# A convolution by five products: the last product added onto the third one in PSUM

## The reference

```python
def _L1_conv_ref(x, w1, w3, w5, wd, wf):
    x1 = _conv(x, w1, padding=[(0, 0), (0, 0)])
    x2 = _conv(x, w3, padding=[(1, 1), (1, 1)])
    x3 = _conv(x, w5, padding=[(2, 2), (2, 2)])
    x4 = _conv(x, wd, padding=[(2, 2), (2, 2)], dilation=(2, 2))
    out = jnp.concatenate([x1, x2, x3, x4], axis=1)
    return _conv(out, wf, padding=[(0, 0), (0, 0)])
...
x = x + _L0_conv_ref(_gn(x), ...)
x = x + _L1_conv_ref(_gn(x), ...)
```

## Time and profile before

| | us |
|---|---|
| Median of three runs | 1710.36 |
| The three runs | 1708.89, 1710.36, 1710.79 |
| Span of the profiled execution | 1706.1 |

### The profile page before, as it was taken

The page is one execution under the profiler, slowest core; times in us unless marked ns, Lnnn a source line. Parts: engine busy times, 40 slices in busy tenths (PEclk is TensorE's granted clock), DMA queues, the critical chain, the costliest instruction groups (busy, mean ns, idle before and its releaser), DMA issues.

```text
span 1706.1 us, 38231 instructions
## 1 busy us (share of the span) xinstructions
PE 1652.5 (97%) x13285; PEld 1552.1 (91%) x13285; DVE 1488.7 (87%) x1964; ACT 1022.2 (60%) x1665; POOL 579.8 (34%) x398
## 2 busy tenths in 40 slices
PE   6999999999999999999999999999999999999998
PEld 6989959999999996999999996899999999599998
DVE  6788879999888859999978886999988887799997
ACT  4856576555385658545546666755446566765551
POOL 4999931222281003232247002123326400312222
PEclk9999979999999997999999999899999999799999
DMA  7012115666502201666630220366661121055553
GB/s 192 0 47 65 38 32 136 177 164 172 153 2 61 69 19 44 157 167 172 169 95 15 69 65 1 87 165 175 167 165 46 35 73 41 1 133 139 135 144 104
DMA packets 105017, 166.01 MB, mean 97 GB/s; under 512 B 40266, under 2 KB 78763, under 8 KB 104780
## 3 DMA queue, kind: packets, MB, share of 16 engines
q1 hardware_dynamic: 81772, 138.95, 32.0%
q10 hardware_dynamic: 23168, 26.04, 4.7%
HBM read 52.20 MB, written 25.17 MB: 45 GB/s over the span
## 4 chain that ended last, share of the span: by engine, by line
PE 84%; DVE 7%; issue 4%; ACT 3%; DMA 1%; DVEq 0%; SPq 0%; POOL 0%; ACTq 0%; POOLq 0%
PE ps L957 41%; PE ps L796 12%; PE ps L817 8%; PE ps L819 7%; PE ps L818 7%; PE ps L845 3%; PE ps L879 3%; PE ps L952 1%; PE ps L752 1%; ACT region L1178 1%; DVE region L1706 1%; DVE region L1676 1%; ACT region L1111 1%; DVE X L1514 1%; DVE region L1673 1%
## 5 line engine op out<-in xcount | busy, mean ns | idle before, releaser
L957 PE MATMUL ps<-region,W 128*96 128x256 f16 (+2 forms) x7140 | 800.7, 270 | 10.0 <-DMA region<-region 5.4
L957 PEld LDWEIGHTS ps<-region,W 128*96 128x96 f16 (+1 forms) x7140 | 771.3, 122 | 31.8 <-issue 14.8
L1428 DVE TENSOR_TENSOR region<-V,band 128x2322 f32<-128x2322 f32 (+2 forms) x104 | 257.8, 2488 | 59.5 <-PE ps L819 56.1
L1178 ACT ACTIVATE region<-region 96x1584 f16<-96x1584 f32 (+2 forms) x80 | 98.4, 1272 | 309.1 <-DVE region L1610 309.1
L701 POOL TENSOR_TENSOR region<-region 96x528 f32<-96x528 f32 (+1 forms) x72 | 92.0, 1282 | 445.9 <-DVE region L1676 328.4
L817 PE MATMUL ps<-region 128*128 (+1 forms) x1152 | 228.1, 280 | 10.4 <-DVE region L1428 4.5
L819 PE MATMUL ps<-region 128*128 (+1 forms) x1152 | 222.8, 275 | 0.0
L818 PE MATMUL ps<-region 128*128 (+1 forms) x1152 | 222.2, 274 | 0.0
L1706 DVE SCALAR_TENSOR_TENSOR region<-ps,small,region 96x768 f32<-96x768 f32 (+1 forms) x220 | 203.7, 988 | 12.1 <-PE ps L957 10.4
L796 PE MATMUL ps<-proj,region 96*128 96x240 f32 x1024 | 209.3, 367 | 0.6 <-DVE region L1402 0.6
L796 PEld LDWEIGHTS ps<-proj,region 96*128 96x128 f32 x1024 | 194.8, 191 | 14.1 <-DVE region L1402 1.0
(11 more groups left out here) (234 smaller groups left out, 2199.8 us busy)
## 6 DMA issues: line engine op xcount, KB each, us to landing
region<-region SPq DMA_DIRECT2D x104, 247.5 KB, 3.9
region<-in_x_dram SPq DMA_DIRECT2D x128, 192.0 KB, 2.3
out_dram<-region SPq DMA_DIRECT2D x40, 576.0 KB, 4.2
region<-region ACTq DMA_DIRECT2D x72, 247.5 KB, 2.4
X<-in_x_dram SPq DMA_DIRECT2D x30, 576.0 KB, 6.2
region<-region SPq DMA_DIRECT2D x32, 247.4 KB, 4.9
X<-in_x_dram SPq DMA_DIRECT2D x19, 384.0 KB, 10.6
region<-region SPq DMA_DIRECT2D x24, 185.6 KB, 3.7
```

The lines of the kernel that those rows point to most:

```text
L957: last = mm(o, w, src, start=k == 0, stop=k == len(steps) - 1, skip_group_check=split and ck > 0)
L1178: act.activation(dst[0:C, a:e, x:z], src, ACT.Copy, scale=1.0 if whole else col(SA)).then_inc(s_h, 1)
L1428: v.tensor_tensor(T[:, i, 3 * c:3 * c + m].rearrange("p m (i j) -> p m i j", j=3), taps.broadcast_to([P, m, BW // 3, 3]), mask.broadcast_t ...
```

## The change

The weights of g4 are made 1.5 times as large. g4 then adds onto g2's banks, once VectorE has read g2 for the output rows 0 and 1 out of three; the row 2 takes g2 + 1.5 g4 in one step, with the factor 2/3 that g2 had there, so VectorE's step for g2 in row 2 is gone. The even units use the banks 6 for g0, g2 and g4, the odd ones 0; g1 has 2 for itself and g3 has 4. The waits of PE, ACT and DVE are counted anew, with 10 steps of a unit in place of 11. g4's low matmul takes 128 rows; the rows 64 to 127 of its weights are zero. ScalarE's first copy moves from behind the two sums to ahead of them. POOL's weight split has one more step, the factor 1.5.

```diff
-    BANKS = ((0, 2, 0, 4, 6), (2, 0, 2, 4, 6), (0, 2, 0, 4, 2))
+    PAIRS_OF = ((6, 2, 6, 4, 6), (0, 2, 0, 4, 0))
...
-        NPL, NH, NL, NCV, NACC = 8, 8, 4, 5, 11
+        NPL, NH, NL, NCV, NACC = 8, 8, 4, 5, 10
...
                 columns(0, h[0])
-                columns(2, h[2])
+                step(pool.tensor_scalar(early, h[2], 1.5, None, ALU.mult))
+                columns(2, early)
...
-                        pe.wait_ge(s_acc, (b * UNITS - 1) * NACC + (5, 9, 8, 0)[i] + START)
+                        if b:
+                            pe.wait_ge(s_acc, (b * UNITS - 1) * NACC + (-2, 2, 7, 8)[i] + START)
...
+                            if not first:
+                                pe.wait_ge(s_acc, (n - 2) * NACC + 8 + START)
+                        elif g == 1:
                             pe.wait_ge(s_acc, (n - 1) * NACC + 2 + START)
-                        elif g == 1:
-                            pe.wait_ge(s_acc, (n - 1) * NACC + 5 + START)
                         elif g == 2:
                             pe.wait_ge(s_t1, n + 1 + START)
                         elif g == 3:
-                            pe.wait_ge(s_acc, (n - 1) * NACC + 8 + START)
-                        elif last_unit:
-                            pe.wait_ge(s_acc, n * NACC + 2 + START)
-                        else:
-                            pe.wait_ge(s_acc, (n - 1) * NACC + 9 + START)
+                            pe.wait_ge(s_acc, (n - 1) * NACC + 7 + START)
+                        elif g == 4:
+                            pe.wait_ge(s_acc, n * NACC + 4 + START)
...
+                            opens = g < 4 and (g != 2 or column // BANK not in cleared)
+                            cleared.add(column // BANK)
...
                             if ck == 0:
-                                rows = 64 * len(rts)
-                                steps.append((wp[0:rows, p, :], window(lo, rows, 0, 0)))
+                                steps.append((wp[:, p, :], window(lo, P, 0, 0)))
...
-                                last = mm(o, w, src, start=k == 0, stop=k == len(steps) - 1, skip_group_check=split and ck > 0)
+                                last = mm(o, w, src, start=opens and k == 0, stop=k == len(steps) - 1,
+                                          skip_group_check=g in (2, 4) or split and ck > 0)
...
                         plain(hi, 1)
                         plain(hi, 0)
+                        between()
                         act.wait_ge(s_pl, later(b, u) * NPL + START)
                         sums(hi, 0)
                         sums(hi, 1)
...
                     act.wait_ge(s_cv, n * NCV + 1 + START)
-                    act.wait_ge(s_acc, (n - 1) * NACC + 7 + START)
+                    act.wait_ge(s_acc, (n - 1) * NACC + 6 + START)
...
                     def midway():
-                        if whole > 1:
-                            first_point(m, i, BPU)
                         if ahead:
                             rows_normed(m + 2, ahead)
...
-                    highs(m + 1, 1 - i, whole, midway)
+                    highs(m + 1, 1 - i, whole, midway, lambda: first_point(m, i, BPU))
...
                     step(1, 2, OSC_THIRD, 1)
-                    step(2, 2, OSC_THIRDS, 2)
...
-                    step(2, 4, OSC)
+                    step(2, 4, OSC_THIRDS)
```

More of the change, by code:

```diff
@@ L146, in build_program, with product_at, product @@
         ps = ctx.enter_context(nc.psum_tensor("ps", [P, 8, BANK], f32))
+        products = ps[0:C].rearrange("p b n -> p (b n)")
+        def product_at(i, g):
+            return PAIRS_OF[i][g] * BANK
+        def product(i, g, blocks):
+            at = product_at(i, g)
+            return products[:, at:at + 3 * KCOL].rearrange("p (c n) -> p c n", c=3)[:, :, 0:blocks * HC]
         pq = region[:, 0:2 * AR * CO].rearrange("p (i r c) -> p i r c", i=2, r=AR)
@@ L336, in build_program @@
         N_TURNED = 3 * (3 + 2) + 1
-        N_SPLIT = 12 + NRT * 6 + 2
+        N_SPLIT = 13 + NRT * 6 + 2
         NPOOL = 18
@@ L886, in _, with unit @@
                 keep_warm(0, 22)
-                def unit(u, i, k2, first, blocks, last_unit=False, halves=False):
+                def unit(u, i, k2, first, blocks, halves=False):
                     n = b * UNITS + u
@@ L892, in unit @@
                     for g, p in enumerate(POINTS):
-                        bank = BANKS[2 if last_unit else i][g]
+                        place = product_at(i, g)
                         if g == 0:
@@ L924, in unit @@
                         split, late = g == 0 or (first or halves) and g == 2, []
+                        cleared = set()
                         for c, ck in enumerate((1, 2, 0)):
-                            o = ps[0:C, bank:bank + 2, :].rearrange("p b n -> p (b n)")[:, ck * KCOL:ck * KCOL + blocks * HC]
+                            column = place + ck * KCOL
+                            o = products[:, column:column + blocks * HC]
+                            opens = g < 4 and (g != 2 or column // BANK not in cleared)
+                            cleared.add(column // BANK)
                             def window(t, rows, second, x):
@@ L964, in _ @@
                     unit(k2 * 2 + 1, 1, k2, False, BPU)
-                unit(UNITS - 1, 0, (UNITS - 1) // 2, False, LASTB, True)
+                unit(UNITS - 1, 0, (UNITS - 1) // 2, False, LASTB)
                 assert st.n == NPST
@@ L1161, in rows_normed, with highs @@
                                    ACT.Identity, bias=col(SBI), scale=col(SA)).then_inc(s_y2, 1)
-                def highs(u, i, whole, midway):
+                def highs(u, i, whole, midway, between=None):
                     n = b * UNITS + u
@@ L1231, in first_point @@
                     n = b * UNITS + u
-                    bank = BANKS[i][0]
                     act.wait_ge(s_cv, n * NCV + 1 + START)
-                    act.wait_ge(s_acc, (n - 1) * NACC + 7 + START)
-                    act.activation(acc[:, 1, :, 0:blocks * HC],
-                                   ps[0:C, bank:bank + 2, :].rearrange("p b n -> p (b n)")[:, 0:3 * KCOL]
-                                   .rearrange("p (c n) -> p c n", c=3)[:, :, 0:blocks * HC],
+                    act.wait_ge(s_acc, (n - 1) * NACC + 6 + START)
+                    act.activation(acc[:, 1, :, 0:blocks * HC], product(i, 0, blocks),
                                    ACT.Copy, scale=col(OSC_MHALF)).then_inc(s_t1, 1)
@@ L1695, in lows @@
                         sums(1, 4)
[L1697 to L1700, removed]
                 def first_rows(u, i, blocks):
@@ L1726, in last_rows @@
                     dve.wait_ge(s_cv, n * NCV + 4 + START)
-                    dve.wait_ge(s_acc, n * NACC + 7 + START)
+                    dve.wait_ge(s_acc, n * NACC + 6 + START)
                     step(0, 3, OSC_HALF)
                     dve.wait_ge(s_cv, n * NCV + 5 + START)
-                    step(2, 4, OSC)
+                    step(2, 4, OSC_THIRDS)
                 def outputs(u, blocks, rows):
@@ L1741, in middle_outputs @@
                     n = b * UNITS + u
-                    dve.wait_ge(s_acc, n * NACC + 5 + START)
+                    dve.wait_ge(s_acc, n * NACC + 4 + START)
                     dve.wait_ge(s_out, n * 16 + START)
@@ L1746, in outer_outputs @@
                 def outer_outputs(u, blocks):
-                    dve.wait_ge(s_acc, (b * UNITS + u) * NACC + 9 + START)
+                    dve.wait_ge(s_acc, (b * UNITS + u) * NACC + 8 + START)
                     outputs(u, blocks, slice(0, 3, 2))
@@ L1777, in _ @@
                 outer_outputs(UNITS - 2, BPU)
-                first_rows(UNITS - 1, 2, LASTB)
-                dve.wait_ge(s_acc, (b * UNITS + UNITS - 1) * NACC + 5 + START)
+                first_rows(UNITS - 1, 0, LASTB)
+                dve.wait_ge(s_acc, (b * UNITS + UNITS - 1) * NACC + 4 + START)
                 rows = X[:, (UNITS - 1) * UR * W:].rearrange("p (r j c) -> p c r j", j=HC, c=2)
@@ L1786, in _ @@
                 middle_outputs(UNITS - 1, LASTB)
-                last_rows(UNITS - 1, 2, LASTB)
+                last_rows(UNITS - 1, 0, LASTB)
                 outer_outputs(UNITS - 1, LASTB)
```

## The result

The changed kernel takes 1698.98 us (median of five runs, 1698.17 to 1701.03). The kernel before, run beside it, takes 1709.94 us. The ratio is 0.9939, with a 95% interval of 0.9927 to 0.9951: 11 us faster. The forecast was 1697.6 us, with a range of 1694 to 1705.

A forecast was written before the change was run, and what follows sets the result against it. VectorE's loop was taken to set PE's pace; 1706.1 us of span less 12.8 us (3.2 us an image, four images) gives 1693.3, plus 4.3 us from span to median makes 1697.6 us; range 1694 to 1705.

The forecast's parts named there:

- VectorE's loop bounded the kernel before: Steady units before: VectorE releases ScalarE's first copy, which releases PE, so PE runs at VectorE's pace, 18.95 us a unit.
- The 64-row matmul costs 0.26 us: PE, low matmul of g4: three steps around it take 0.59 us where 0.33 is regular; 128 rows save 0.26 us.
- The rival that this cost isn't its height: PE, 64-row matmul: its extra cost has another cause and stays, units 18.79 us, total 1707 us; chance 0.05.
- PE's unit becomes 18.53 us: Steady units after the change: PE needs 167 matmuls by 0.111 us, 18.53 us, and becomes the bound.
- VectorE has 0.51 us a unit to spare: VectorE's loop: one step of 0.926 us less takes it from 18.95 to 18.02 us, 0.51 us below PE's unit.
- The loop of the output's write: VectorE's middle outputs waiting for the previous unit's write: a loop of 17.5 us, below 18.53, so it costs nothing.
- g4's new wait is paid once: PE, g4 waiting for VectorE's two reads of g2: 2.6 us idle in unit 0 of each image, nothing afterwards.
- The rival of shared banks paid in every unit: PE at g4: both reads of g2 stand bare each unit, 20.5 us a unit, total 1758 us; chance 0.02.
- The clock falls at unit 0: Rival, PE behind g4's new idle: half of some 20 us lost, 10 us an image, 1718 to 1738 us; chance 0.06.
- The copy moved, and the looser waits: ScalarE's first copy ahead of the sums, and looser waits at g0, g1 and the next image: both cost nothing.
- POOL's extra step: POOL's weight split, once: one step of 2.7 us, covered by 14.74 us of POOL idle behind the split.
- The sum: Per image -0.2, +3.3 from eight units, +0.1: 3.2 us gained; four images 12.8 us.

The follow-up runs named there:

- the copy back: Changed kernel with ScalarE's first copy back behind the two sums: 1698.34 us, ratio 0.9927; with matmuls filling unit 0's idle as well, 1694.88 us.
- the warming matmuls: Changed kernel with identity matmuls into a free bank ahead of g4's wait in unit 0: 1696.70 us, ratio 0.9917; again 1695.99 us, ratio 0.9915.
- POOL's other order: Changed kernel with POOL's second difference issued ahead of its residual instead of behind it: 1702.59 us, ratio 0.9957.
- VectorE's first rows ahead: Changed kernel with VectorE's four steps for unit 0 moved ahead of its last two low parts of unit 1: 1704.06 us, ratio 0.9970.

## Why the prediction was right, and where a term was off

- **VectorE's loop bounded the kernel before, and the two edits need each other.** Right. With the 128 rows alone the units stay at 18.95 us; with the VectorE step alone (the 64 rows back) they are 18.79.
- **The 64-row matmul costs 0.26 us.** Right: 18.79 us with it, 18.53 without, in every steady unit. The rival that this cost isn't its height is out.
- **PE's unit becomes 18.53 us.** Right to the hundredth.
- **VectorE has 0.51 us a unit to spare.** Wrong, and the one step of the working that failed. The step priced the removed instruction by its own 0.926 us and moved everything behind it forward at its old duration. The plane step then lay 0.63 us beside POOL's difference and grew by 0.49 us. Where POOL isn't beside it, the loop is the 18.02 us of the forecast (18.03 in image 1). The gaps of 0.5 us on VectorE that were to show the step right aren't there, except where it waits for the write of the output (0.56 us above) and, with 0.28 us, in the last image with the copy back. The time was right all the same, because VectorE's 18.51 us are still just below PE's 18.53. The forecast had no ground for these 0.02 us, so that much is luck. The loop of the output's write, counted at nothing, is late by such amounts too. PE doesn't see it in the first profile of the changed kernel; with the warming matmuls it did, by 0.20 and 0.36 us in two units.
- **g4's new wait is paid once.** Right: 2.6 us of idle forecast in image 0, 2.43 measured, and 1.59 to 2.30 in the others; the wait at unit 1's g2 went as forecast, and no wait at g4 breaks PE from unit 1 on in the changed kernel's first profile. The reason given, that VectorE gains 0.51 us a unit, isn't the one: as I read it, and no run tests it by itself, two loops of equal length keep the phase that unit 1 leaves them. POOL's other order, which puts VectorE 0.21 us above PE, shows the wait in steady units at once. The rival of shared banks paid in every unit is out. The Trainium skill's "Perfetto Trace Analysis", Optimizing Tensor Performance, Matmuls, would have groups rotate through banks; in the changed kernel three of the five products share one pair, and PE is busy 148.24 of 148.24 us, because other products lie between them.
- **The clock falls at unit 0.** This rival, with a chance of 0.06, came true in its mechanism and not in its price, and with it one of the forecast's signs of being wrong, a clock below 1.00 behind unit 0. It was priced at half of some 20 us, from the stretch in the attention; the stretch here is 3.4 us, 1.6 us an image, in one to three images of four. In the six traces with this idle and no warming matmuls it fell in 12 of 24 images; in the four where warming matmuls shorten the idle it fell in none of 16. So the fall comes with the long idle, but not each time. The Trainium skill's "TensorE: Matmul & The Clock Gate", Part 1, says that idling brings the low clock back, and the traces agree in 12 of the 17 images whose idle at g4 was 1.88 us or longer.
- **The copy moved, and the looser waits.** Nothing, as forecast. **POOL's extra step** took 3.6 us against 2.7, and POOL still idles 13.19 us behind the split against 14.74, so its cover held.
- **The sum.** 3.2 us an image were forecast; an image whose clock stays up gains 205.4 - 202.35 = 3.05 us, so 12.2 us in all. The falls take back 1.6 to 4.7 us. The three medians of the changed kernel, each against the kernel before beside it, give 11.0, 13.2 and 10.2 us, while the convolutions of the three traces gain 7.8, 11.0 and 8.1 us. The other 2 to 3 us aren't explained by the change: the span without the convolutions is 884.1 to 887.3 us in the thirteen traces, whatever the kernel, and 884.5 us in the only trace of the kernel before, whose execution was 2 us below its median. So it is in part luck that the median came within 1.4 us of a sum without the falls. The 4.3 us that the forecast carried from span to median were 1.7 us around the span, and the rest was the spread of executions.

## What to carry to other kernels

When two engines are both near the bound, price the edit on each alone, and expect the gain only from both: here 0.7 and 2.1 us apart, 11 together. When a step goes away, everything behind it moves; look which work of another engine it comes to lie beside, because durations read from the old place needn't hold in the new one. A wait that is paid once per image can still cost more than its idle, if the clock falls behind it, and a few matmuls without use in that idle were a cheap cure here.

## What the runs showed of the hardware that I had not expected

- **A step of VectorE with both inputs in SBUF and a POOL subtraction hold each other up: the one that begins second ends as if it had waited for the first.** In six overlaps the second took its usual time plus the overlap, less some 0.14 us. The wide plane step (1.80 us alone) takes 2.29 us with 0.63 us beside a POOL subtraction and 1.93 us with 0.27 us. With VectorE's first rows ahead it begins 1.25 us before the end of POOL's first difference and takes 2.91 us. POOL's second difference begins 1.70 us before the end of that plane step and takes 2.87 us, 1.31 us elsewhere. L1616 begins 1.13 us before the end of that difference and takes 1.70 us, 0.70 us elsewhere. With POOL's other order VectorE's two steps of 96x512 begin 0.85 us before the end of POOL's pair and take 2.00 us, 1.29 us elsewhere, while POOL, which began first, keeps its 1.31 us a difference. Steps that read one input from PSUM aren't held: L1712's step (L1706 before) takes 1006 to 1008 ns in every kernel, though POOL's residual runs beside it. The Trainium skill, "SBUF — State Buffer", Who interferes with whom, says that a DVE instruction with two SBUF inputs contends with a GpSimd instruction that reads SBUF, and one with at most one, outside the two-port modes, doesn't; the runs agree on both. By that rule the failed step could have been foreseen.

With VectorE's first rows ahead:

```profile
278.55 1.30 POOL L712 TENSOR_TENSOR region<-region 96x528 f32<-96x528 f32 x1 [32.69 <-DVE region L1687]
279.81 2.87 POOL L712 TENSOR_TENSOR region<-region 96x528 f32<-96x528 f32 x1
```

With POOL's other order:

```profile
329.23 2.58 POOL L712 TENSOR_TENSOR region<-region 96x528 f32<-96x528 f32 x2 [12.27 <-DVE region L1687]
330.96 2.00 DVE L1742 TENSOR_TENSOR region<-region 96x512 f32<-96x512 f32 x2
```

- **The granted clock doesn't answer the same idle in the same way.** Image 0 idled 2.43 to 2.45 us at g4 in four traces, and the clock fell; it idled 2.42 us in two others, and it didn't. 1.88 and 2.00 us were followed by a fall, 2.21 and 2.25 us in images 2 and 3 of one execution weren't. The seven idles at g4 of 1.15 to 1.78 us, in the traces without warming matmuls, never were. What decides stays open.
